# LSTM cells on one core: lookup ahead of the sum in the small cell, digits made there, forget gate ahead of the second lookup, tanh first in the large cell, three one-hot buffers

## The reference

```
def lstm_last(x, Wx, Wh, b):
    def step(carry, xt):
        h, c = carry
        g = xt @ Wx + h @ Wh + b
        i, f, gg, o = jnp.split(g, 4, axis=-1)
        c = sigmoid(f) * c + sigmoid(i) * tanh(gg)
        h = sigmoid(o) * tanh(c)
        return ((h, c), None)
...
m_from = lstm_last(base_emb[from_seq], seq_Wx, seq_Wh, seq_b)
m_to = lstm_last(base_emb[to_seq], seq_Wx, seq_Wh, seq_b)
def enc(ne, fe, Wx, Wh, b, nums, fr):
    return lstm_last(concatenate([ne[nums], fe[fr]]), Wx, Wh, b)
nwf = vmap(enc)(...)                      # 11 features
return relu(feats @ reduce_W + reduce_b)
```

## Time and profile before

| | |
|---|---|
| median of 3 runs | 1712.03 us (1711.87 to 1713.39) |
| profiled execution | 1714.94 us, its span 1713.1 us |
| busy in the span | PE 1610.2 (94%), DVE 1509.0 (88%), ACT 1314.0 (77%), POOL 955.3 (56%) |
| granted TensorE clock, mean | 0.989 of full speed |
| DMA queue of SP | 439.63 MB, 81.8% of 16 engines' span |

### The profile page before, as it was taken

The page is one execution under the profiler, slowest core; times in us unless marked ns, Lnnn a source line. Parts: engine busy times, 40 slices in busy tenths (PEclk is TensorE's granted clock), DMA queues, the critical chain, the costliest instruction groups (busy, mean ns, idle before and its releaser), DMA issues.

```text
span 1713.1 us, 57020 instructions
## 1 busy us (share of the span) xinstructions
PE 1610.2 (94%) x23780; PEld 619.1 (36%) x23780; DVE 1509.0 (88%) x1573; ACT 1314.0 (77%) x2011; POOL 955.3 (56%) x473
## 2 busy tenths in 40 slices
PE   3799999999999999999999999999999999999997
PEld 0233333333333333333333333333333333333334
DVE  6788988989988989988989988988988988988984
ACT  4577777877777877777877778877778877778874
POOL 1445666776666776666754444554444554444553
PEclk8899999999999999999999999999999999999999
DMA  8678789898889898889788789899889888788870
GB/s 285 223 253 261 248 263 276 264 276 271 256 268 284 250 284 260 270 264 284 251 287 262 260 263 277 260 275 267 273 265 280 256 277 274 256 267 273 248 241 24
DMA packets 165793, 444.19 MB, mean 259 GB/s; under 512 B 45728, under 2 KB 103584, under 8 KB 132640
## 3 DMA queue, kind: packets, MB, share of 16 engines
q1 hardware_dynamic: 162112, 439.63, 81.8%
q0 software_dynamic: 2560, 0.15, 0.6%
q10 hardware_dynamic: 864, 0.75, 0.1%
HBM read 423.42 MB, written 6.82 MB: 251 GB/s over the span
## 4 chain that ended last, share of the span: by engine, by line
PE 53%; DVE 17%; ACT 15%; issue 9%; POOL 2%; DVEq 0%; POOLq 0%; ACTq 0%
PE e_ps L479 16%; PE ab L619 11%; PE f_ps L619 9%; PE ab L511 7%; DVE kept L493 7%; ACT gate L673 5%; DVE f_ps L705 5%; DVE seq_c L710 4%; ACT f_ps L671 3%; PE ab L425 3%; ACT tanh_c L664 3%; PE ab L560 2%; POOL ig L697 2%; ACT f_ps L673 2%; PE ab L570 2%
## 5 line engine op out<-in xcount | busy, mean ns | idle before, releaser
L697 POOL TENSOR_TENSOR ig<-gate 128x1024 f32<-128x1024 f32 x192 | 411.9, 2145 | 696.3 <-ACT seq_x L432 293.7
L479 PE MATMUL e_ps<-hot,tab 128*32 128x512 bf16 x8448 | 527.5, 384 | 61.6 <-DVE kept L493 56.8
L493 DVE SCALAR_TENSOR_TENSOR kept<-high,cst,e_ps 128x1024 f32<-128x1024 uint8 x352 | 449.1, 1276 | 49.6 <-PE e_ps L479 43.8
L619 PE MATMUL ab<-seq_h,seq_wh 64*64 64x512 f32 x3024 | 401.2, 590 | 0.0
L479 PEld LDWEIGHTS e_ps<-hot,tab 128*32 128x32 bf16 x8448 | 214.0, 97 | 486.8 <-issue 342.7
L469 DVE TENSOR_SCALAR hot<-low,cst 128x4096 bf16<-128x4096 bf16 x256 | 320.6, 1281 | 13.2 <-PE e_ps L479 13.2
L731 POOL TENSOR_TENSOR seq_h<-gate,tanh_c 128x1024 f32<-128x1024 f32 x128 | 308.9, 2414 | 31.8 <-ACT tanh_c L664 31.6
L673 ACT ACTIVATE gate<-ab,nwf_bias 128x512 f32<-128x512 f32 (+2 forms) x384 | 188.4, 553 | 166.2 <-PE ab L570 103.0
L671 ACT ACTIVATE gate<-ab 128x1024 f32<-128x1024 f32 x256 | 262.5, 1026 | 17.6 <-PE ab L619 8.8
L664 ACT ACTIVATE tanh_c<-seq_c 64x512 f32<-64x512 f32 (+1 forms) x384 | 241.9, 630 | 29.8 <-POOL nwf_h L731 22.1
L664 ACT ACTIVATE gate<-ab 64x512 f32<-64x512 f32 (+1 forms) x384 | 228.5, 595 | 9.4
(11 more groups left out here) (99 smaller groups left out, 1809.1 us busy)
## 6 DMA issues: line engine op xcount, KB each, us to landing
low<-low_digits SPq DMA_DIRECT2D x256, 1024.0 KB
low<-low_bytes SPq DMA_DIRECT2D x96, 512.0 KB
tok<-seq_tokens SPq DMA_DIRECT2D x128, 384.0 KB
high<-high_digits SPq DMA_DIRECT2D x1408, 32.0 KB
nwf_hq<-nwf_h SPq DMA_DIRECT2D x62, 128.0 KB
raw<-in_indices SPq DMA_DIRECT2D x32, 176.0 KB
low_digits<-low_of SPq DMA_DIRECT2D x32, 88.0 KB, 3.2
nwf_hq<-nwf_h SPq DMA_DIRECT2D x62, 32.0 KB, 3.0
```

What stands on the lines that cost most here:

```text
L479: last = nc.tensor.matmul(e_ps[32 * g:32 * g + 32, i, :], tab[:, part, 2 * m + ty, :], hot[:, p % HOT_RING, g, i, :], start=(part == 0), s ...
L493: nc.vector.scalar_tensor_tensor(out=kept[:, p % KEPT_RING, :, :], in0=wanted, scalar=cst[:, C_HIGH:C_HIGH + 1], in1=e_ps[:, :, :], op0=AL ...
L619: last = nc.tensor.matmul(flat(bank)[to:to + 64, cols], lhs(rows, half, block), rhs(rows, block, a, b), start=start, stop=stop)
L697: nc.gpsimd.tensor_tensor(ig[:, cols], gates[0][:, n % 2, cols], gates[1][:, n % 2, cols], ALU.mult).then_inc(ig_ready, 1)
```

## The change

No instruction is added or removed; the order on the engines, one ring and one cell for the digits change.
- HOT_RING goes from 2 to 3, and a constant COMPARED = 2 keeps how far the compares run ahead.
- The digits of round r are made in the small cell of step r-3 (c2), behind its compare, and not in the large cell of step r-2 (c5), between its two compares.
- TensorE: in a seq cell gate 0, first lookup, gate 1, forget gate, sum, second lookup, token lookup, gate 3. In the small cell lookup ahead of the sum. The uses of `ab` (USES) follow.
- ScalarE: in a seq cell the forget sigmoid comes right after gate 1, ahead of the stores; in the large cell tanh of c4 comes ahead of gates 0 and 1.

```diff
-ROUND_AT = {(0, 3)[_r - 1] if _r < 3 else NUMBER["nwf", _r - 2, 0]: _r for _r in range(FIRST_ROUNDS, NWF_T)}
+ROUND_AT = {(0, 3)[_r - 1] if _r < 3 else NUMBER["nwf", _r - 3, 1]: _r for _r in range(FIRST_ROUNDS, NWF_T)}
...
-LOW_RING, HIGH_RING, HOT_RING, KEPT_RING = 4, 5, 2, 5
+LOW_RING, HIGH_RING, HOT_RING, KEPT_RING = 4, 5, 3, 5
+
+COMPARED = 2
...
-        USES += [("gate", _n, 0), *_x, ("gate", _n, 1)]
+        USES += [("gate", _n, 0), ("gate", _n, 1), *_x]
...
                     for p in compared[:2]:
                         compare_pair(dve, p)
-                        if p == compared[0] and n in ROUND_AT and CELLS[n][0] == "nwf":
-
-                            make_digits(dve, ROUND_AT[n])
+                    if n in ROUND_AT and CELLS[n][0] == "nwf":
+                        make_digits(dve, ROUND_AT[n])
...
+                    if CELLS[n][0] == "seq":
+                        activate(act, n, 0)
                         if n:
                             tanh_of(act, n - 1)
+                        activate(act, n, 1)
+                        activate_f(act, n)
                         store_sums(act, n)
-                    activate(act, n, 1)
-                    if not is_seq and n < LAST:
-                        tanh_of(act, n - 1)
-                    if later_seq(n) is not None:
-                        seq_store_x(act, later_seq(n))
-                    activate_f(act, n)
+                        if later_seq(n) is not None:
+                            seq_store_x(act, later_seq(n))
+                    else:
+                        store_sums(act, n)
+                        if CELLS[n][2] == 0 or n == LAST:
+                            tanh_of(act, n - 1)
+                        activate(act, n, 0)
+                        activate(act, n, 1)
+                        if CELLS[n][2] and n < LAST:
+                            tanh_of(act, n - 1)
+                        activate_f(act, n)
...
                         gate(pe, n, 0)
                         for p in pairs[:1]:
                             look_up(pe, p)
+                        gate(pe, n, 1)
+                        gate(pe, n, FORGET)
                         sums(pe, n)
-                    else:
+                    elif large:
                         sums(pe, n)
                         for p in pairs[:1]:
                             look_up(pe, p)
+                    else:
+
+                        for p in pairs[:1]:
+                            look_up(pe, p)
+                        sums(pe, n)
                         if not large:
                             gate(pe, n, 0)
+                            gate(pe, n, 1)
```

More of the change, by code:

```diff
@@ L862, in _ @@
                     seq_compare(dve, s)
-                for p in range(HOT_RING):
+                for p in range(COMPARED):
                     compare_pair(dve, p)
@@ L868, in _ @@
                     pairs = PAIRS_AT[n]
-                    compared = [p + HOT_RING for p in pairs if p + HOT_RING < ALL_PAIRS]
+                    compared = [p + COMPARED for p in pairs if p + COMPARED < ALL_PAIRS]
                     for p in pairs[:1]:
@@ L917, in _ @@
                     for p in PAIRS_AT[n][:2][-1:]:
-                        pool.wait_ge(hot_ready, min(p + HOT_RING + 1, ALL_PAIRS))
+                        pool.wait_ge(hot_ready, min(p + COMPARED + 1, ALL_PAIRS))
                     input_product(pool, n)
@@ L940, in _ @@
                 for n in range(NCELLS):
-                    is_seq = CELLS[n][0] == "seq"
-                    if n == LAST:
-                        tanh_of(act, n - 1)
-                    if not is_seq:
-                        store_sums(act, n)
-                    activate(act, n, 0)
-                    if is_seq:
+                    if CELLS[n][0] == "seq":
+                        activate(act, n, 0)
                         if n:
                             tanh_of(act, n - 1)
+                        activate(act, n, 1)
+                        activate_f(act, n)
                         store_sums(act, n)
-                    activate(act, n, 1)
-                    if not is_seq and n < LAST:
-                        tanh_of(act, n - 1)
-                    if later_seq(n) is not None:
-                        seq_store_x(act, later_seq(n))
-                    activate_f(act, n)
+                        if later_seq(n) is not None:
[9 more added lines that the diff above has]
+                        activate_f(act, n)
                     activate(act, n, 3)
@@ L982, in _ @@
                             look_up(pe, p)
+                    else:
+                        for p in pairs[:1]:
+                            look_up(pe, p)
+                        sums(pe, n)
                         if not large:
                             gate(pe, n, 0)
+                            gate(pe, n, 1)
                     if large:
                         gates_of_large(pe, n, 0, 1)
-                    else:
-                        gate(pe, n, 1)
                     for p in pairs[1:]:
@@ L995, in _ @@
                     else:
-                        gate(pe, n, FORGET)
+                        if CELLS[n][0] == "nwf":
+                            gate(pe, n, FORGET)
                         gate(pe, n, 3)
```

## The result

The changed kernel takes 1738.82 us (median of 4 runs, 1735.55 to 1740.04); the kernel before took 1712.71 beside it (4 runs). The ratio is 1.0146, 95% interval 1.0126 to 1.0166. I had forecast 1690 and faster; it is slower, in the direction and by the mechanism of rival A.

A forecast was written before the change was run, and what follows sets the result against it. VectorE was taken to limit c0, c1, c3, c4; TensorE c2 and, with ScalarE, c5's start. Rounds of 51.43 - 0.3 - 0.3 + 0.2 = 51.0 early, 50.3 late, save 22.5: 1690 us, forecast 1684 to 1697, range 1670 to 1724.

The forecast's parts named there:

- rival A: In c2 the digits meet GpSimd's new_h of c1: 2.2 us in each of 29 rounds, 1754 us; chance 0.20.
- the unknown cost: GpSimd's product and new_h beside the digits in c2: taken as 0, with +2.2 us kept for the range.
- Digits out of c5 and tanh first: In c5 the scale starts earlier: 0.3 us in an early round; late rounds gain 0.7 more.
- The ring: Three one-hot buffers: a compare no longer waits for a lookup, -0.3 us a round.
- The order of the seq cells: Forget gate ahead of second lookup, sum behind it: TensorE's wait goes but VectorE was never idle there; worth 0.
- The lookup ahead of the sum in c2: Small gates, then first lookup of c3 and keep(5), come later: +0.2 us a round.
- The sum for a late round: Rounds without gathers, from round 15 on: 51.0 - 0.7 = 50.3 us.
- The sum over the run: 13 early rounds 5.6, 15 late 15.6, first three and last about 1.5: 22.5 us less in all.
- The sum for an early round: Round with gathers: 51.43 - 0.3 - 0.3 + 0.2 = 51.0 us.
- Rival B: TensorE is the bound after all and its waits go: 56.8 us less, 1655 us; chance 0.08.
- Rival C: No gain: later second lookups make VectorE wait in c0 and c3, 0.4 to 0.8 a round, 1703 to 1713; chance 0.12.

The follow-up runs named there:

- the version without the meeting: Changed kernel plus one wait on GpSimd: in c2 new_h of c1 is held back until the digits are made; 1693.15 us, ratio 0.988.
- the best version: Changed kernel with the digits ahead of the compare in c2 and gathers only in c0, c1, c3 and c5, no wait added; 1679.36 us, ratio 0.9804.

## Why the prediction was wrong

**The step that failed** is the one on the unknown cost: "By my count the last port-hungry pair starts 0.1 us before new_h is ready, and new_h waits instead. I take 0 and keep +2.2 for the range." The three times that it was made of were right to 0.1: the digits start at K+5.76 (forecast K+5.73), the product at K+6.20 (K+6.24), new_h at K+7.94 (K+8.04). I had also seen that "the product can hold up the digits by at most about 0.9", and it did, by 0.7. Even the start of the last pair was nearly as counted: L363 at K+7.91, 0.03 ahead of new_h, where I had 0.1. What failed is the conclusion, that new_h then waits for the pair. It came between the two: L364 starts 0.26 us behind L363, at K+8.17, and so 0.23 behind new_h, which held it to its own end. My own numbers said so: digits that are held 0.7 to 0.9 end at K+8.4 to K+8.6, and their last instruction, 0.34 long, starts at K+8.1 to K+8.3, behind new_h at K+8.04. An instruction that is ahead keeps GpSimd off for its own length only, not for that of the next. By the measured numbers rival A should have had the larger chance.

**The mechanism, shown.** Keeping new_h behind the digits gives 1693.15, keeping the digits ahead of both GpSimd instructions 1695.1, both from 1738.8; putting the digits back in c5 1709.7. In the timelines above the held instruction ends 0.1 to 0.2 us after the GpSimd instruction each time. The Trainium skill, "SBUF — State Buffer", section "Who interferes with whom", says that whichever of the two issues first holds the shared ports to its end. The traces agree: L340 has two SBUF inputs (1.02 us), L364 is a cast (2.51), and L358 in the run with only the digits moved is a tensor_scalar (2.31). The other order shows too: the new_h that starts 0.03 us behind L363 takes 2.54 us, against 2.38 in the run where it is held back.

**The size.** Rival A had 2.2 us a round, 1754 in all; VectorE did lose 2.2 at L364. But the round lost 1.69 late (52.00 against 50.31) and 1.26 early (52.71 against 51.45). Late, the version without the meeting waits 0.29 before a keep of c4 that the changed kernel does not have. Early, in the changed kernel, the gather behind new_h starts at 856.73 and takes 0.98 us, not 3.65, since VectorE has not come to the compares of c3; that saves the 0.74 by which the add of c3 is late with the held new_h (1.02 less 0.28). Some 0.1 to 0.2 us a round is left without a name.

**Term by term, where the meeting is away.**
- Digits out of c5 and tanh first, 0.3 early and 1.0 late: right. With tanh behind, 0.27 of it is missing late; with the digits in c5 nothing of it is there in the length of the round.
- The ring, "-0.3": wrong by itself, it gains nothing (1715.8, ratio 1.0004 to 1.0022). In the new order it holds 39 us, which I did not see: I counted the second lookup against its keep, and not against the compare that needs its buffer.
- The order of the seq cells, "worth 0": 0.2 us a round, 6.5 in all, from the forget sigmoid, of which I had said that "the scale there is not what c2 waits for". Not more, since the adds wait for GpSimd's product in its place, which I had at nothing.
- The lookup ahead of the sum in c2, "+0.2": the small gates came within 0.13 of where I said, but that was not its worth. It brings keep(4) and with it the digits forward; without it a round is 0.86 longer late and 1.15 early.
- The gather behind new_h of c2, held up beside the compares of c3, was missing: +0.4 in each early round.
- The sum for a late round, 50.3, is met (50.31), in part by luck. By stretches of the round at 1052.04: S to the scale of c5 10.71 (forecast 10.7), from there to K 16.04 (16.12), K to keep(5) 9.54 (9.67), to the last keep of c4 12.70 (12.54), to S 1.32. The +0.2 came out at +0.07 and the ring's -0.3 at -0.14, with 0.28 before an add and 0.29 before a keep as new waits; the two errors cancel.
- The sum over the run has a slip: 5.6, 15.6 and 1.5 make 22.7 and not 22.5. It changes nothing.
- The sum for an early round, 51.0, is 0.4 short (51.45). With the 13 early rounds that is 6 us; the version without the meeting measured 1693.15 against my 1690, so the other small errors give half of it back.

Rival B has something for it: in the best version TensorE is busy for 49.53 of 50.32 us, so little is left there for VectorE to give. No run here takes VectorE's work away to show which of the two is then the bound. Rival C did not occur: VectorE has no new idle time before its second keeps. Its new idle time is before the adds.

## What to carry to other kernels

Before you move small VectorE instructions (casts, integer tensor_scalar, two inputs in SBUF) into a gap, lay GpSimd's instructions over that gap with their starts: each of them can cost the length of the GpSimd instruction, which here was seven times its own. An instruction that starts just ahead of GpSimd's does not protect the one behind it. Carry every hold that you grant forward to the start of the instruction behind it, and when a margin is smaller than that hold, take the dear case as the forecast. Where the two must share a gap, put the short VectorE work first or let GpSimd wait for it: one wait, or three moved lines, turned +1.5% into -1.2% or -1.0%.

## What the hardware showed that I had not expected

- A gather issued by GpSimd (0.98 us) took 3.26 to 3.65 beside the compares of VectorE in the version with the held new_h. Behind the one of 3.65 GpSimd's product came 0.7 us late; behind the one of 3.26 it came no later, since the product waits for the same compares. It is not only GpSimd's arithmetic that is held. The Trainium skill, "SBUF — State Buffer", section "Who interferes with whom", says that GpSimd is starved of port time when a transfer that it issues stalls beside a VectorE instruction; the trace agrees.
- Where such a gather stood ahead of the first gates of c5, TensorE was through them 0.7 us later, without a wait on GpSimd at that place in the program. The idle time lies within the gates, before a weight load that waits only for an earlier matmul of TensorE itself; a late round has no such row:

```profile
803.38 0.15 PEld L562 LDWEIGHTS ab<-nwf_x,large_w 32*32 32x32 f32 x8 [0.65 <-PE ab L572]
```

What joins the two was not found out; moving the gather to another cell took the 0.7 away.
